# A state-space layer whose outputs are made transposed, with its decays in two rounded parts, and int8-style weights rounded in transposed form

## The reference

```python
# fifth sublayer: state space (cut)
zxbcdt = u @ W_in                         # 512 -> 1024 (z) + 1280 (x, B, C) + 16 (dt)
xBC = silu(conv(xBC))                     # 4 taps, depthwise
dt = softplus(dt + dt_bias);  A = -exp(A_log)
y, _ = ssd(x * dt, A * dt, B, C)          # y[l] = sum_{s<=l} (C[l].B[s]) exp(sum of A*dt over s+1..l) x[s]*dt[s], 16 heads of 64
y = (y + x * D) * silu(z)
y = y * rsqrt(mean(y*y) + eps) * norm_scale
x = x + y @ W_out
# sixth sublayer: feed-forward with rounded activations and weights (cut)
w1q = quant_dequant(w_gate_up, axis=-1)   # scale = max|row| / 127, round(v / scale) * scale
gate, up = split(xq @ w1q.T);  h = silu(gate) * up
x = x + quant_dequant(h) @ quant_dequant(w_down).T
```

## Time and profile before

| | us |
|---|---|
| three runs, median (lowest, highest) | 1077.73 (1073.68, 1078.02) |
| the profiled execution | 1079.65 |
| its span, first to last instruction | 1077.9 |
| PE busy | 1020.7 (95%) |
| DVE busy | 734.0 (68%) |
| ACT busy | 572.2 (53%) |
| POOL busy | 269.1 (25%) |
| granted TensorE clock, mean | 0.988 |

### The profile page before, as it was taken

One profiled execution on the slowest core, in us unless ns is written; L12 is line 12 of the kernel. 1 busy time (PEld: TensorE's weight loads), 2 busy tenths in 40 slices (PEclk: granted clock), 3 DMA queues, 4 the chain that ended last, 5 costly groups with the idle time before them and its releaser, 6 DMA issues.

```text
span 1077.9 us, 18635 instructions
## 1 busy us (share of the span) xinstructions
PE 1020.7 (95%) x6849; PEld 809.4 (75%) x6849; DVE 734.0 (68%) x1441; ACT 572.2 (53%) x1227; POOL 269.1 (25%) x209
## 2 busy tenths in 40 slices
PE   8989989999998899999999999999999999898996
PEld 5545789999996666687888878787877879667743
DVE  3656455556644889788887878888788876554534
ACT  3345344444434210677767677776767769343413
POOL 6810144444332200022220212222022011104411
PEclk9999999999999999999999999999999999999998
DMA  9450075566623232111020211202021126404010
GB/s 276 113 237 1 13 252 207 209 211 216 226 72 100 86 101 81 48 30 33 8 77 4 54 33 31 57 5 71 13 61 42 42 65 148 143 6 161 1 64 20
DMA packets 72253, 97.49 MB, mean 90 GB/s; under 512 B 35665, under 2 KB 53233, under 8 KB 71026
## 3 DMA queue, kind: packets, MB, share of 16 engines
q1 hardware_dynamic: 72178, 96.49, 28.6%
HBM read 91.58 MB, written 4.90 MB: 89 GB/s over the span
## 4 chain that ended last, share of the span: by engine, by line
PE 79%; DVE 12%; ACT 5%; issue 2%; DMA 1%; POOL 1%; SPq 0%; DVEq 0%; ACTq 0%; POOLq 0%
PE PS L1551 16%; PE PS L1424 12%; PE PS L1540 10%; PE PS L1528 8%; PE PS L1443 5%; PE PS L1513 4%; DVE scores L1078 2%; PE PS L1565 2%; PE PS L1272 2%; PE PS L1637 2%; ACT scores L788 1%; PE PS L1720 1%; PE PS L1646 1%; PE PS L1324 1%; PE PS L1483 1%
## 5 line engine op out<-in xcount | busy, mean ns | idle before, releaser
L1133 DVE TENSOR_TENSOR pL<-PS,pH 128x512 fp32r<-128x512 f32 x256 | 175.9, 687 | 60.1 <-ACT pH L812 59.2
L812 ACT ACTIVATE pH<-PS 128x512 fp32r<-128x512 f32 x256 | 151.7, 595 | 100.4 <-PE PS L1540 100.4
L788 ACT ACTIVATE scores<-scores,nmX 128x512 f32<-128x512 f32 x256 | 185.1, 723 | 18.5 <-DVE nmX L1082 18.5
L1078 DVE TENSOR_SCALAR_CACHE_REDUCE scores<-PS 128x512 f32<-128x512 f32 x256 | 172.6, 682 | 20.4 <-PE PS L1528 20.2
L1551 PE MATMUL PS<-pH,kvH 128*128 128x256 f32 x512 | 164.5, 321 | 6.6 <-ACT xnT L797 6.6
L1540 PE MATMUL PS<-ident,scores 128*128 128x128 f32 x1024 | 157.1, 276 | 1.0 <-DVE pL L1133 1.0
L1551 PE MATMUL PS<-pL,kvH 128*128 128x256 f32 x512 | 144.0, 281 | 0.0
L1551 PE MATMUL PS<-pH,kvL 128*128 128x256 f32 x512 | 143.7, 281 | 0.0
L1540 PEld LDWEIGHTS PS<-ident,scores 128*128 128x128 f32 x1024 | 117.3, 140 | 32.0 <-issue 14.4
L1551 PEld LDWEIGHTS PS<-pH,kvH 128*128 128x128 f32 x512 | 96.7, 189 | 10.8 <-issue 10.6
L1551 PEld LDWEIGHTS PS<-pL,kvH 128*128 128x128 f32 x512 | 97.2, 190 | 0.0
(11 more groups left out here) (309 smaller groups left out, 2273.9 us busy)
## 6 DMA issues: line engine op xcount, KB each, us to landing
rawG<-in_wg SPq DMA_DIRECT2D x16, 768.0 KB, 5.7
rawU<-in_wu SPq DMA_DIRECT2D x16, 768.0 KB, 7.1
rawD<-in_wd SPq DMA_DIRECT2D x16, 768.0 KB, 6.1
xn<-in_w SPq DMA_DIRECT2D x11, 512.0 KB, 3.7
wblk<-blocks SPq DMA_DIRECT2D x4, 1056.0 KB, 8.1
wb<-w_rows SPq DMA_DIRECT2D x32, 128.0 KB, 3.3
wqX<-in_wqX SPq DMA_DIRECT2D x16, 256.0 KB, 2.6
woX<-in_woX SPq DMA_DIRECT2D x8, 512.0 KB, 4.8
```

Source lines behind the costliest of these rows:

```text
L788: act.activation(at, at, ACT.Exp, bias=nmX[:, p % 2, h, q:q + 1], accum_out=csum[:, p % 2, NT * h + q, c:c + 1]).then_inc(exp_done, 1)
L812: act.activation(pH[:, i % 4], PS[:, 2 + i % 2, :].rearrange("p (k t) -> p k t", t=T), ACT.Copy).then_inc(pH_ready, 1)
L1078: dve.tensor_scalar(sp_[:, h, q, c * CH:(c + 1) * CH], PS[:, 4 * q + h, :], 1.0, None, ALU.mult, ALU.max, accum_out=cmax[:, h, q, c:c + 1] ...
L1133: dve.tensor_tensor(pL[:, i % 4], PS[:, 2 + i % 2, :].rearrange("p (k t) -> p k t", t=T), pH[:, i % 4].bitcast(F32), ALU.subtract).then_in ...
```

## The change

**State space, transposed.** z is made with channels on partitions as x is, in 4 steps between the x steps (`XZORDER`); C·B follows early. Heads go in pairs (`m`, 8 of them). `log_decay(m)` takes two heads: the weights that PE holds are now the constant triangle `afterR` and `onesR`, and what streams is `upto` times the decay, split in a high and a low part in fp32r (`avH`, `avL`), so one pass for each part. `ua` is made by POOL for the first token half and by ACT (`weighted_late`) for the second, six pairs ahead. `ssm_out(m)` gives y transposed: 64 channels of each head on its own half of the partitions, in one bank a pair. DVE adds the skip and multiplies by silu(z) (`yt`, `yz`), ACT scales (`yn`) and squares (`y2`), POOL sums the squares over the pairs, and PE projects pair m-1 right after `ssm_out(m)`. The mean of squares comes from small matmuls with a column of ones.

**Rounding, transposed.** The 15 row jobs give only scales and their inverses (`i_rows`). They are in chunks 1, 4 and 7, w2 first, so they end in period 4. Then 17 jobs load the weights in transposed layout (`w1t`, `w2t`, laid out beforehand), POOL multiplies by the broadcast inverses, adds and subtracts the rounding constant, and SP stores 128-partition strips in `turned`. They start five jobs behind the maxima. The state-space layer no longer turns or copies weights: one load of `turned` in four parts gives them. `win` is loaded after the loop over periods.

```diff
+ROWS_AT = (1, 4, 7)
+LAG = 5
+XZORDER = (("x", 4), ("x", 0), ("x", 1), ("z", 0), ("x", 2), ("z", 1), ("x", 3), ("z", 2), ("z", 3))
 # DVE, long attention
-                        if c == 1 and e % 2:
-                            row_max(2 * p, e // 2)
-                        if c == 6 and e % 2 and p + 1 < XP:
-                            row_max(2 * p + 1, e // 2)
+                        if c in ROWS_AT and e % 2 and len(ROWS_AT) * p + ROWS_AT.index(c) < JOBS:
+                            row_max(len(ROWS_AT) * p + ROWS_AT.index(c), e // 2)
 # SP, after the loop over the periods (was inside it, in period 7, ahead of load_out)
+            sp.wait_ge(sX_ps, XP * SLOTS)
+            sp.dma_start(win[:, 0:KT - 1], ...)
+            sp.wait_ge(wint_ready, len(TURNED))
+            store_turned(*TURNED[-1])
+            sp.wait_ge(wint_stored, 16 * len(TURNED))
             sp.dma_start(win[:, KT - 1], ...)
 # PE, two heads of log decays, and one pair's outputs
+                for j in range(2):
+                    pe.matmul(PS[:, bank, :], afterR[:], ua[:, m % UA, j, 0:2 * T], start=(j == 0), stop=False)
+                for j in range(2):
+                    pe.matmul(PS[:, bank, :]...[:, :, P:T], onesR[:], ua[:, m % UA, j, 2 * T:]..., start=False, stop=(j == 1))
+                for j in range(2):
+                    mm = pe.matmul(PS[:, bank + 1, 0:T], afterR[:], ua[:, m % UA, j, 2 * T:], start=(j == 0), stop=(j == 1))
+                for h in range(2):
+                    pe.matmul(PS[HP * h:HP * h + HP, 4 + b, 0:T], xdt[:, 0, ...], mh[:, b, h * T:(h + 1) * T], ...)
+                for h in range(2):
+                    mm = pe.matmul(PS[HP * h:HP * h + HP, 4 + b, P:T], xdt[:, 1, ...], mh[:, b, 2 * T + h * P:2 * T + (h + 1) * P], ...)
 # PE, the pairs
+            for m in range(IT):
+                ssm_out(m)
+                if m:
+                    pe.wait_ge(yn_ready, m)
+                    for t in range(NT):
+                        mm = project(m - 1, t)
+                    mm.then_inc(o_done, 1)
+                if m + 2 < IT:
+                    log_decay(m + 2)
+            stay_awake(6, 7)
+            project(IT - 1, 0); ...four matmuls for the mean of squares...; project(IT - 1, 1)
 # DVE, the pairs
+            masked(0)
+            masked(1)
+            for m in range(IT):
+                dve.wait_ge(y_ps, m + 1)
+                step(dve.scalar_tensor_tensor(yt[:, m % 2], act_[:, m], dskip[:, m:m + 1], PS[:, 4 + m % 2, 0:T], ALU.mult, ALU.add))
+                dve.tensor_tensor(yz[:, m % 2], yt[:, m % 2], zs[:, m], ALU.mult).then_inc(yz_ready, 1)
+                if m + 2 < IT:
+                    masked(m + 2)
 # ACT, the pairs
+            for m in range(IT):
+                act.activation(yn[:, m % 2], yz[:, m % 2], ACT.Copy, scale=ns[:, m:m + 1]).then_inc(yn_ready, 1)
+                act.activation(y2[:, m % 2], yz[:, m % 2], ACT.Square).then_inc(y2_ready, 1)
+                if m + 2 < IT:
+                    exp_pair(m + 2)
...
```

More of the change, by code:

```diff
@@ L429, in _, with rows, columns @@
+            def rows(n):
+                sp.wait_ge(winv_ready, n + 1)
+                store_scales(n)
+                if n + 1 < JOBS:
+                    load_rows(n + 1)
+            def columns(j):
+                kind, n = TURNED[j]
+                if j:
+                    sp.wait_ge(wint_ready, j)
+                    store_turned(*TURNED[j - 1])
+                sp.wait_ge(scale_stored, STORED[DT if kind == 2 else DT + n + 1])
+                load_turned(kind, n)
             load_rows(0)
@@ L587, in _ @@
             pool.wait_ge(qr_ready, XP)
[L588 to L591, removed]
+            for p in range(XP):
+                if p + 2 < XP:
+                    low_parts(p + 2)
+                for n in range(len(ROWS_AT) * p, len(ROWS_AT) * (p + 1)):
+                    if 0 <= n - LAG < len(TURNED):
+                        round_columns(n - LAG)
             rstd(4)
@@ L869, in _ @@
[L869 to L875 removed]
+                if k:
+                    silu_pair(k - 1, xs_before[-1])
@@ L1225, in _ @@
+            dve.wait_ge(late_pe.sem, late_pe.at("ss", 1))
+            step(dve.tensor_scalar(ss[:], PS[:, 6, 0:NT], 1.0 / DI, LN_EPS, ALU.mult, ALU.add))
             dve.sem_inc(late_dve.sem, 1)
@@ new lines, in ssm_out @@
+            def ssm_out(m):
+                b = m % 2
+                pe.wait_ge(mh_ready, m + 1)
+                wait(pe, yz_ready, m - 1)
+                for h in range(2):
+                    pe.matmul(PS[HP * h:HP * h + HP, 4 + b, 0:T], xdt[:, 0, (2 * m + h) * HP:(2 * m + h + 1) * HP], mh[:, b, h * T:(h + 1) * T],
+                              start=True, stop=False, skip_group_check=True)
+                for h in range(2):
+                    mm = pe.matmul(PS[HP * h:HP * h + HP, 4 + b, P:T], xdt[:, 1, (2 * m + h) * HP:(2 * m + h + 1) * HP], mh[:, b, 2 * T + h * P:2 * T + (h + 1) * P],
+                                   start=False, stop=True, skip_group_check=True)
+                mm.then_inc(y_ps, 1)
@@ L1719, in _ @@
-                for t in range(NT):
-                    mm = pe.matmul(PS[:, t, :], yT[:, m, t * P:(t + 1) * P], wout[:, m, :], start=(m == 0), stop=(m == IT - 1))
+                ssm_out(m)
[7 more added lines that the diff above has]
+            stay_awake(6, 7)
+            pe.wait_ge(yn_ready, IT)
```

416 lines of the change are left out of this document (211 added, 205 removed).

## The result

| us | before | after |
|---|---|---|
| median of the runs (lowest to highest) | 1077.88 (1073.68 to 1080.17), 4 runs | 1114.8 (1110.92 to 1118.0), 4 runs |
| ratio of after to before | | 1.0346, 95% interval 1.0297 to 1.0394 |
| span of the profiled execution | 1077.9 | 1109.2 |
| up to the first keys of the long attention (PE) | 438.29 | 436.52 |
| from there to the dt matmuls of the state space | 498.96 | 561.71 |

The differences are -1.8, +62.75, -28.6 and -1.1 us, together the 31.3 us of the spans. The forecast of -26.0 for the state-space layer was met and more. The loss lies in the long attention, where the forecast had -1.5.

A forecast was written before the change was run, and what follows sets the result against it. PE's own work was taken to bound the state-space loop, with the projection serial behind it. State space -26.0, long attention -1.5, `win` +0.5 give -27.0: 1079.65 to 1052.65, less 1.92 for the median, 1050.7 us; range 1045 to 1054.

The forecast's parts named there:

- the first term of the part on the long attention: Long attention: periods 0 to 4, with row jobs in chunks 1, 4 and 7, stay unchanged, +0.3 for wider w2.
- rival E: Long attention: DVE waits for rows issued behind tiny stores, decided from a landing of 16 us; +40, 1091 us; chance 0.02.
- State space, -26.0: State-space layer: transposed z, paired heads, no block transposes, projection inside the loop; -26.2 us by sum, taken as -26.0.
- A pair: State-space loop: a pair's round trip over DVE and ACT takes 3.75 us, longer than PE's own 3.44.
- rival D: State-space loop: two heads' output matmuls don't run side by side, 0.75 becomes 1.5; +3, 1054 us; chance 0.03.
- Rival C: State space: DVE and POOL block each other, lengthening masks or `yz`; 4 to 8 us, 1055 to 1059; chance 0.10.
- `win`, +0.5: Load of `win`, moved behind `woX`: lands just in time before the state space; taken as +0.5 us.
- Rival A: Ahead of the state space: `win` comes late by up to 8 us, 1058 us; chance 0.12.
- Row jobs: Long attention: +0.3 for wider w2, PE's wait of 0.85 goes in periods 5 and 6; sum given as -1.5.
- rival B: Long attention: row jobs push the ends of the periods, +7 instead of -1.5, 1059 us; chance 0.08.
- The criterion "the time outside 937 to 1037 moves by more than 3 us": Outside the state-space stage: the forecast is wrong if time outside 937 to 1037 us moves by over 3 us.

The follow-up runs named there:

- e3: The changed kernel without any tiny store, scales and inverses read from a constant input: 1055.67 us, 0.9792 of the kernel before.
- e2: The changed kernel without the stores of the scales, those of the inverses kept: 1063.56 us in one run.
- e1: The changed kernel with the loads of the next rows issued before the stores of scales and inverses: 1095.48 us, 1.0138 of the kernel before.
- e10: e9 with ACT squaring a pair's output only after the exponential of the next pair but one: 1051.89 us, 0.9749 of the kernel before.
- e9: e7 with the row maxima in chunks 1, 4 and 6 instead of 1, 4 and 7: 1051.96 us in one run.
- e7: The changed kernel with scales and inverses transposed on DVE, each store 4 pieces of 128 bytes: 1061.86 us, 0.9862 of the kernel before.
- e9r: e9 again, unchanged, in five rounds: 1053.76 us, 0.9779 of the kernel before.
- e5: The changed kernel with the four tiny stores of a w1 job merged into two of 256 pieces of 4 bytes: 1124.49 us in one run.
- b1: The kernel before with scales and inverses stored in four stores of 128 4-byte pieces ahead of the next row load: 1153.94 us in one run.
- b2: The kernel before with inverses stored too, four tiny stores after each job, behind load and blocks: 1090.83 us in one run.
- e8: e7 with the row maxima in chunks 1, 3 and 5 instead of 1, 4 and 7: 1054.62 us, 0.9775 of the kernel before.

## Why the prediction was wrong

**The step that failed** is the first term of the part on the long attention together with the price in rival E. "Periods 0 to 4 stay as they are" rests on rows that land in 3.7 us. That landing was measured in a kernel where the load is issued ahead of everything. The change issues it behind two or four stores, which the text names, and the row was carried over all the same. Behind four stores the rows landed in 17 to 18 us, and the first four periods took 61 us more. Rival E named the mechanism of the late rows, and it was given 0.02, with the note "Nothing in the trace points to it, except that many small pieces slowed one transfer by 9 us". The recorded text has no price for the stores beyond "some 4" us for the job's end and them. E's condition ("a landing of 16") is not tested: no run here has landings of 16 us without stops. From 3.9 us without them (e3) to 11.4 behind 256 pieces (e2) are 0.029 us a piece, and to 17.5 behind 512 (after) 0.027. The trace of the kernel before alone has no row for it: its 26 stores of scales stood last, where nobody waited. The prediction should have kept both ends in its sum, as it did for `win`, since by its own reading small pieces had already cost 9 us there.

**What E had not** are the stops. With a landing of 17.5 its own arithmetic gives 4 x (17.5 - 9) = 34 us and 1084, 31 short of the measured 1114.8. The runs part the two costs: e1, with the stops alone, is 40 us over e3, which has neither, and the late rows add 19 more. (After has fewer stops than e1, 20.1 us by the same count against 44.5, so the two overlap and don't add strictly.)

**The other terms.**

- State space, -26.0: -28.6. From the start of dt to the fillers 71.75 were forecast, 69.39 measured; z ended 34.45 us after dt's start (at 1032.68), forecast 35.45.
- A pair: 3.75 by a round trip over DVE and ACT, with PE's work at 3.44. It is 3.64, and PE's work is what sets it: no gap on PE in the rows above, and e10 takes 0.40 out of the round trip for nothing. That 3.75 came close is luck: it was the price of the wrong bound. The log decays and the projection took 2.84 us by the starts (1048.09 to 1050.93), not 2.69; the outputs 0.80, not 0.75. The heads' outputs do run side by side, so rival D falls.
- Rival C: the masks in the loop (0.96, where 1.0 was taken) lost nothing to POOL, whose sums of squares fall elsewhere. The second mask, ahead of the loop, took 1.79 beside POOL's `ua` (1037.24): rival C is real there, and costs 0.8 us once.
- `win`, +0.5: nothing. From the last values to dt are 11.45 us before (925.8 to 937.25) and 11.4 after (986.8 to 998.23). Its large part landed in 12.5 us, forecast 10.3 + 2. Rival A falls.
- Row jobs: +0.3 for the wider w2 and -0.85 twice were forecast (-1.4; the text has -1.5). Without late rows (e3) it is +1.3 in four periods, -0.4 and -0.7 in the next two: +4 instead of -1.5. This is rival B, which had +7, and e9 puts it on the half job in chunk 7. "Takes back the 1.0 that DVE gains" was the wrong balance: behind chunk 7 there is no slack, in chunk 6 there is.
- The criterion "the time outside 937 to 1037 moves by more than 3 us" was met at once.

With the stores mended (e7) and the job out of chunk 7 (e9r) the change gives 1053.8, 3 us from the forecast of 1050.7, and 24.8 under the kernel before beside it, where 27.0 were forecast.

## What to carry to other kernels

A column of scalars stored from 128 partitions is 128 pieces of 4 bytes: count a DMA's pieces, not only its bytes, and ask what stands behind it in the queue. A landing time of the trace holds only for the place in the queue at which it was measured; when an edit moves a load behind something new, bound its landing from both sides before saying that it is covered. Turn such a column into rows on chip first (one 32x32 block transpose on DVE was enough) and keep side jobs out of the last chunk before a point that all engines wait for.

## What was not expected of the hardware

- 512 pieces of 4 bytes (2 KB in all) held up a load by 13.6 us (17.5 against 3.9). The pieces were not what took the time: they were through in 2 us, and the packets of 2 KB behind them took 1.23 us each (624 to 625 us) instead of 0.08. 16 pieces of 128 bytes, the same data, held the load up by 0.2.
  The Trainium skill (DMA: Bandwidth & Descriptors, Specifications) says that below 512 B the DMA engine reads, modifies and writes back. The runs agree that small pieces are dear. They don't tell whether a piece of 128 bytes is cheaper than one of 4: at 0.027 us a piece 16 pieces would cost 0.4 us, and 0.2 were measured.
- While loads were so held up, PE's semaphores were raised up to 6.1 us after the work was done by the trace (e5, 718.18 to 724.32), and ACT and DVE stood and waited for them. By the count used for e1 there are 11 such waits in e1, 7 in e5, 5 in b1, 4 after and 3 in b2, all kernels with 512 tiny pieces for a job of w1, and none in the kernel before, e2, e3, e7, e8, e9, e9r and e10. In the stretches in question the trace has no record of any semaphore, of engines or of DMAs, for 2 to 9 us (581.97 to 587.54 in e1), though PE works on for part of them on tiles that DVE made meanwhile. So signals of DVE reached PE without a record, and the recording itself is disturbed too. What holds them up isn't settled.
  The Trainium skill (Runtime: NRT & Kernel Launch, Instruction fetch mechanics) says that each engine fetches its instructions by a DMA queue of its own in blocks of 256. That would be a way for a blocked DMA engine to stop ACT. The trace of e1 speaks against it: ACT began 0.02 us after the semaphore that it waited for was raised, and it executed 1735 instructions in all (1251 of them work), at most seven blocks, which is too few for 11 stops in one stage.
- A DVE operation on two columns (L1171) took 1.55 us, while POOL's addition L616 (618.40 to 620.29) ran beside it. The same operation takes 0.17 in nine of its 15 executions, and 0.56 to 1.55 in the six that began over 0.5 us before an operation of POOL ended; each of the six ended 0.02 to 0.03 us after POOL's:

```profile
618.77 1.55 DVE L1171 TENSOR_SCALAR wscale<-wmax 128x2 f32<-128x2 f32 x1
620.35 0.17 DVE L1173 RECIPROCAL winv<-wscale 128x2 f32<-128x2 f32 x1
```
